# A graph and expert kernel on one core: the return of the experts' rows and the graph setup in one stage, and the first stage's bulk loads issued by SyncE

## What is computed

```python
x = x + L0_gnn(layernorm(x), edges)      # 40000 edges: MLP on 8 edge features, gather, products, sum by receiver
x = x + L0_ffn(layernorm(x))             # 4 groups x 8 experts, 2 groups and 2 experts each are chosen
x = x + L1_gnn(layernorm(x), edges)      # two attention convolutions (4 heads x 256), then fc
x = x + L1_ffn(layernorm(x))             # 16 experts, each takes its 156 best nodes
```

```python
h = edge_feats
for W in (W_mlp1, W_mlp2, W_mlp3):
    h = SILU_2MOM * silu(h @ W / sqrt(W.shape[0]))
```

```python
moe = moe + iw[:, e] * (h @ W2[g, e] + b2[g, e])
y = _layernorm(z + moe, gln_g[g], gln_b[g])
out = out + gw[:, g] * y
```

## Time and profile before

| | us |
|---|---|
| median of 3 runs | 2354.38 |
| lowest and highest run | 2353.44, 2356.39 |
| profiled execution | 2353.07 |
| its span | 2351.4 |

### The profile page before, as it was taken

How to read it: one execution, slowest core, us unless ns; L and a number is a source line. 1 busy time by engine, 2 the same in 40 slices (tenths; PEclk the granted TensorE clock), 3 DMA queues, 4 the chain that set the end, 5 groups by cost and what they waited for, 6 DMA issues and landing times. The chain is left out here.

```text
span 2351.4 us, 36494 instructions
## 1 busy us (share of the span) xinstructions
PE 2003.0 (85%) x11260; PEld 1288.4 (55%) x11261; DVE 1513.0 (64%) x2331; ACT 1118.3 (48%) x2278; POOL 748.9 (32%) x629
## 2 busy tenths in 40 slices
PE   5899999999997738999975497999999999980997
PEld 2444444444445727777732444777344777540997
DVE  1289999999995774333348865777763778428011
ACT  5777777777773404555510313666001676210332
POOL 4287777777770012444453000000000000000453
PEclk9989999999998957999988598999999999995998
DMA  5565555555551423788544313000012100221794
GB/s 160 168 170 157 154 155 154 153 154 152 155 155 53 95 85 129 268 261 265 174 129 132 96 43 115 22 22 1 18 43 81 64 22 1 104 100 46 221 277 94
DMA packets 200741, 285.12 MB, mean 121 GB/s; under 512 B 116698, under 2 KB 128677, under 8 KB 196543
## 3 DMA queue, kind: packets, MB, share of 16 engines
q0 software_dynamic: 98272, 142.08, 21.2%
q1 hardware_dynamic: 100158, 137.67, 19.0%
q10 hardware_dynamic: 2209, 4.07, 0.5%
HBM read 233.52 MB, written 49.84 MB: 121 GB/s over the span
## 5 line engine op out<-in xcount | busy, mean ns | idle before, releaser
L565 POOL DMA_INDIRECT p_s<-node_table,e_src_rows x320 | 454.5, 1420 | 147.4 <-issue 86.7
L2004 PE MATMUL g_psO<-g_h,g_ring 125*125 125x257 f32 x1600 | 372.4, 388 | 19.7 <-DVE g_ring L2136 10.3
L2004 PEld LDWEIGHTS g_psO<-g_h,g_ring 125*125 125x125 f32 x1600 | 296.6, 190 | 92.1 <-DVE g_stage L2130 26.6
L703 PE MATMUL p_psW<-e_w,p_hid 64*125 64x512 f32 x640 | 275.4, 654 | 50.2 <-ACT z L580 24.7
L622 DVE TENSOR_TENSOR g_b<-z,p_s 125x1536 f32<-125x1536 f32 x160 | 273.6, 1751 | 0.0
L711 PE MATMUL p_psM<-g_b 125*32 125x384 f32 x648 | 249.5, 533 | 11.0 <-DVE p_key L684 5.9
L580 ACT ACTIVATE z<-p_psW 125x512 f32<-125x512 f32 x320 | 187.2, 585 | 147.0 <-PE p_psW L703 139.0
L715 PE MATMUL p_psM<-g_b 125*32 125x256 f32 x648 | 218.8, 422 | 0.0
L714 PE MATMUL p_psM<-g_b 125*32 125x256 f32 x648 | 211.3, 410 | 0.0
L713 PE MATMUL p_psM<-g_b 125*32 125x256 f32 x648 | 193.8, 426 | 0.0
L585 ACT ACTIVATE p_of<-e_node_ids,z 125x314 bf16<-125x314 f16 x320 | 176.2, 551 | 6.8 <-PE p_psC L720 3.1
(11 more groups left out here) (357 smaller groups left out, 3775.2 us busy)
## 6 DMA issues: line engine op xcount, KB each, us to landing
p_ring<-in_L_ffn_weights SPq DMA_DIRECT2D x32, 1025.0 KB
slot_rows<-p_y POOLq DMA_DIRECT2D x70, 256.0 KB
p_w1s<-in_L_ffn_w SPq DMA_DIRECT2D x16, 1024.0 KB
g_a<-in_L_ffn_w SPq DMA_DIRECT2D x16, 1024.0 KB
hidden<-g_b SPq DMA_DIRECT2D x40, 250.0 KB, 3.2
p_hid<-hidden SPq DMA_DIRECT2D x160, 62.5 KB
g_rb<-receiver_rows SPq DMA_DIRECT2D x16, 610.4 KB
p_s<-node_table,e_src_rows POOLq DMA_INDIRECT x320
```

Source lines behind the costliest of these rows:

```text
L565: pool.indirect_dma_start(s[:, g % 4, c, :, :].rearrange("p k u -> p (k u)"), None, node_table, bass.IndirectOffsetOnAxis(ap=src_rows[:, g ...
L703: nc.tensor.matmul(psW[c % 2][0:P, :], hid[part, b, c // 2, :], w4[part, :], start=True, stop=True)\
L2004: last = nc.tensor.matmul(psO[0:P, j, 0:HW], ring[:, i % RING, j * P:(j + 1) * P], h[:, s, hd, :], start=s == 0, stop=s == T - 1)
```

## The change

In prepare, SyncE issues the bulk loads, in portions, each behind the stores of a round; ScalarE issues none. LEAD becomes 5, so that the node tiles go with the rounds 5 to 9.

```diff
-    LEAD = 4
+    LEAD = 5
...
+                    if i == 0:
+                        rows_in(0)
+                        rows_in(1)
+                    if i == 1:
+                        for k in range(2, T // 2):
+                            rows_in(k)
+                    if i == 2:
+                        sp.dma_start(dsts[:], dst.rearrange("(g e) -> g e", e=EG)).then_inc(dst_in, 16)
+                        sp.dma_start(wu[:, 0, :], w_up0).then_inc(up_in, 16)
+                        sp.dma_start(wu[:, 1, :], w_up1).then_inc(up_in, 16)
+                    if i == 3:
...
-                for k in range(T // 2):
-                    act.dma_start(xs[:, 2 * k:2 * k + 2, :], rows[:, 2 * k:2 * k + 2, :]).then_inc(x_in[k], 16)
```

The function combine replaces that block and graph_setup. The stage change with cleared semaphores is now ahead of it. TensorE, ScalarE and VectorE work tile by tile on both:

```diff
+                pe.wait_ge(consts, 2)
+                turn_wide(0)
+                turn_wide(1)
+                offsets(0)
+                for i in range(2, TURNS):
+                    turn_wide(i)
+                turn_counts(0)
+                offsets(1)
+                turn_counts(1)
+                for t in range(T):
+                    sums(t)
+                    gains(t)
+                    if t + 2 < T:
+                        offsets(t + 2)
+                    if t:
+                        turn_rows(t - 1)
+                    if t + 2 < T:
+                        turn_counts(t + 2)
+                turn_rows(T - 1)
...
+                for t in range(T):
+                    if t + 1 < T:
+                        roots(t + 1)
+                    row_root(t)
+                    if t:
+                        take_rows(t - 1)
+                    if t + 2 < T:
+                        take_counts(t + 2)
+                take_rows(T - 1)
...
+                difference(0)
+                difference(1)
+                mix(0)
                 for t in range(T):
+                    if t + 1 < T:
+                        mix(t + 1)
+                    finish(t)
+                    if t + 2 < T:
+                        difference(t + 2)
+                    if 2 <= t < 2 + KD:
+                        v.wait_ge(att_in, 32)
+                        v.wait_ge(ws_in[t - 2], 16)
+                        attention_vectors(nc, v, wa_ok, ws, att, prod, wa, t - 2)
+                    norm(t)
```

The banks: offsets have one pair (in place of two), sums one bank (in place of two), gains one pair as before, the turned rows one, the turned counts two in place of six, so that `turn_counts` waits for ScalarE's copy of its first batch before its third. The mask is made by ScalarE, ahead of the three copies, in another form:

```diff
-                    nc.vector.tensor_scalar(far[:, t, :], rows[:, t % 2, 0:N], 0.0, FAR, ALU.is_equal, ALU.mult)\
...
+                def take_counts(t):
+                    act.wait_ge(looped, t + 1)
+                    nc.scalar.activation(far[:, t, :], rows[:, t % 2, 0:N], ACT.Relu, bias=away[:], scale=FAR)\
...
-        n = tick(nc.vector.tensor_tensor(prod[:, i, :], ws[:, k, :], att[:, i, :], ALU.mult))
-        tick.wait(n)
-        nc.vector.tensor_reduce(wa[:, k, i, :], prod[:, i, :].rearrange("p (h c) -> p h c", h=HEADS),
-                                AX.X, ALU.add).then_inc(wa_ok, 1)
+        for hd in range(HEADS):
+            own = slice(hd * HC_GAT, (hd + 1) * HC_GAT)
+            last = nc.vector.tensor_tensor_reduce(out=prod[:, i, own], in0=ws[:, k, own], in1=att[:, i, own], scale=1.0,
+                                                  scalar=0.0, op0=ALU.mult, op1=ALU.add, accum_out=wa[:, k, i, hd:hd + 1])
+        last.then_inc(wa_ok, 1)
```

479 lines of the change are left out of this document (238 added, 241 removed).

## The result

| | before | after |
|---|---|---|
| median | 2354.38 us | 2370.85 us |
| lowest and highest run | 2349.49, 2356.39 | 2366.00, 2380.46 |
| profiled execution | 2353.07 us | 2366.00 us |
| its span | 2351.4 us | 2364.2 us |

The changed kernel is slower: 1.0089 times the time before, 95% interval 1.0071 to 1.0106. (The ratios of this text are made from all runs of both kernels and are not the quotients of the medians; here that quotient is 1.0070, or 16.5 us, where 1.0089 would be 21.) Its five runs lie 14 us apart, those of before 7. One of the twelve executions of a later run, e8, took 4045 us, which the record calls slow, and its ratio leaves it out.

A forecast was written before the change was run, and what follows sets the result against it. ScalarE was taken to bound the first stage, VectorE the return and graph setup. Joined stage −15.7, planning −1.4 and first part −0.7 sum to −17.8 us, giving 2336.6 us from the median 2354.38; range 2322 to 2347.

The forecast's parts named there:

- First part: First stage, bulk loads on SyncE: earlier start −14.5, stores held up behind x +12.5, end +1.3; sum −0.7 us.
- the tail: End of first stage: with LEAD 5 the last node_table store ends it about 1.3 us later.
- the 113: Start of the edge stage: expected at about 108; before 100 or after 113 us would show the forecast wrong.
- the stores are not held up: First stage, rival: x leaves the stores' share free, the 12.5 us are not given back; 2324 us, 13%.
- Planning: Experts' planning stage: removing the 1.38 us clearing from GpSimd's head gains 1.4 us.
- Joined stage: Return of the experts' rows joined with graph setup: 141.6 us in place of 157.3, gain 15.7 us.
- Lead-in: Start of the joined stage: the old 12.4 us wait for the first gather kept, bounds 11.2 and 15.
- Waits on TensorE: Joined stage: VectorE waits 1.3 us in four tiles, 5; one offsets bank and ordered start, about 3 us.
- Stage change: Semaphore clearing, moved in front of the joined stage: still costs about 1.0 us.
- the 76.0 us of the old tiles: Joined stage: the return's ten tiles take as long as before, 76.0 us.
- The clock falls: Joined stage, rival: TensorE's clock sits at 0.50, tiles take about 14 us each; 2362 us, 5%.
- TensorE's order bounds the joined stage: Joined stage, rival: every tile waits, 2 us more in each of ten; 2345 us, 8%.

The follow-up runs named there:

- e8: e2 with attention vectors and W1 loaded later, counts' loads cut into 112 and 13 rows, gains and sums ahead of turned counts: ratio 0.9990.
- e5: Kernel before with only the first stage's part of the change, each x load cut into 112 and 13 rows: ratio 0.9974.
- e3: Changed kernel with attention vectors and W1 loaded behind the stores of tiles 0 to 3 of the joined stage: 2367.72 us, ratio 1.0054.
- e10: e2 with turned gates and small given 128 rows again, 88 of them zeros: ratio 1.0057.
- e2: Changed kernel with the first stage of the kernel before, so the joined stage alone: 2369.14 us, ratio 1.0054.
- e9: Kernel before with offsets, sums and gains in the return contracting over 40 rows in place of 128: 2372.88 us, ratio 1.0132.
- e13: e12 with TensorE's order of the changed kernel, turned counts ahead of sums and gains: ratio 0.9943.
- e4: Changed kernel with TensorE doing a tile's gains and sums ahead of the turned counts and rows: 2367.37 us, ratio 1.0055.
- e12: e8 with 128 rows in turned gates and small, plus the first stage of e5: ratio 0.9880.

## Why the prediction was wrong

The forecast was 2336.6 us; it came out at 2370.85, outside the range and on the other side.

**First part: right in mechanism, short by one step.** Predicted −14.5, +12.5, +1.3; measured −14.8, +12.1 (the four waits for stores), +1.6 for the tail (109.05 to 114.21, before 105.77 to 109.32). What the sum lacked is a fourth term of 6.0 us, the remainder to +4.9: TensorE, stopped by those waits, came back at 0.55 and 0.62 and made ScalarE wait 1.3 and 0.6 us here and there. The two rounds behind the two long waits show it: without their waits for stores they take 9.1 and 9.2 us (from 33.04 to 49.20, less the 7.08, and from there to the start of the next third layer, less 0.41), where a plain round took 6.13. The prediction put this at nothing. The edge stage began at 114.21, just past the 113 that I had named as a sign of being wrong. Of the rivals, "the stores are not held up" (13%) is refuted, and e5 shows where its 12 us lay.

**Planning: wrong, small.** I subtracted the 1.38 us of a removed instruction on an engine whose head is bound by something else. GpSimd's first select ends 3.7 us after the engine starts, with the clearing ahead of it (842.91, 1.89 us long, 841.12 the start) or without (843.23, 3.33 us, 842.88). The row to ask was the select itself, 1.89 us where its like in the joined stage takes 0.29. What binds it is not shown.

**Joined stage: 141.6 predicted, 169.0 measured** (168.5, and 0.5 for the stage change that the sum counts in). By the terms:
- Lead-in 12.4, measured 23.8 to the first mix: +11.4. I had seen the 4 MB beside the gathers and kept the old 12.4, with 15 as a bound. At the 257 GB/s that the stretch from 1205 to 1212 shows, 4 MB alone are 16 us. The bound was too small for numbers that I had written down myself.
- Second mix: a wait of 8.6 us for gathers, not in the sum at all. I had asked only when the first gather lands. e3 and e8 (12.5 and 19.1 us for both mixes) show that both waits were the loads'.
- Waits on TensorE, predicted 5 and 3, measured 20.5: +12.5. The step that failed is that a tile's TensorE work runs "at the upper clock". In the tile of 1330.03 the gains did take their 1.88 us, but the sums, priced 1.9, took 3.0 (1325.09 to 1328.11) and the turn of the counts 2.5, so VectorE waited 2.7 us and not 1.3; in four tiles, the last two among them (waits of 5.1 and 5.5 us), the gains took 3.62 as well. With 128 rows in the same order (e10) 14.7 us of waits stay, beside 21.0 in e2, so the 40 rows account for 6.2 us of them and the order, with the idle time that it leaves TensorE, for the rest.
- Stage change 1.0, measured 0.5: −0.5. The rest held: 0.35 us per reduction (0.345 from start to start), 10.4 us for a tile without attention vectors and without its wait (10.55 in the sum), 13.15 with (13.35). All of it takes 115.6 us where the sum has 120.2, −4.6: the 76.0 us of the old tiles held 4.0 us of waits of their own (1.94 for a gather, 2.01 for the last gains), which are now among the waits above.

11.4 + 8.6 + 12.5 − 0.5 − 4.6 gives the 27.4 us. Loads are 20.0 of them, so the largest failed step of the whole forecast is the lead-in kept at 12.4 with no second wait.

**The rival nearest to the result was the one that I gave 5%, in part by luck.** "The clock falls" had 2362, by tiles of 14 us; they took 13.4. But it had the old lead-in, and 20.0 us of what came were loads; and with 128 rows in the old order the tiles still take 12.8 us (e10), so their pace is the order's as well as the clock's. I had dismissed the rival by a row that shows 9.3 of 15 us busy at 1.00, as if the busy share decided. e9 refutes that in one line: 15.00 of 15 us busy and 0.50. The diff told it, in `M = WIDE` and `spare[0:WIDE]`, and I had read past them as a saving of space. The Trainium skill, page "TensorE: Matmul & The Clock Gate", section "What's actually happening", says that the gate is set by how busy the engine has been of late. The tiles of e10 agree, where the clock is 0.50 after 3.66 us of idling. By the profile's busy times it is not enough: with 40 rows the clock stayed down through 100 us of full stretches in e9 (1190 to 1290), and the measurement decides.

**"TensorE's order bounds the joined stage"** (8%, 2 us in each tile, 2345) was right as well: 14 us by e13. It and the rows hid each other, since mending either alone left the clock low in part of every tile (e4, e10).

What stays open: why the clock is 0.77 for half of e12's stage with the same 128 rows. Its trace has TensorE idle for 0.71, 1.16 and 1.64 us within one such tile (1238 to 1243) and the clock at 0.50 from 1240 to 1246, which points to idle time; but the transposes fall there too, and none was taken out alone. Also open: why 40 rows keep the clock down for a whole return in e9 and let it rise in six tiles of the changed kernel, where products and transposes over 125 rows stand between; how many rows are needed, since only 40, 125 and 128 ran; why the runs of the changed kernel lie 14 us apart; and the −3.7 us in the other stretches.
